# A graph network on one core: reading the numbers of four tiles with one register load

## The reference, cut to what matters

```python
edge_index = jnp.stack([src, dst])
x = _layernorm(x + _L0_gnn_ref(x, src, dst), axis=-1)                      # segment_sum(x[src], dst)
x = _layernorm(x + _L1_gnn_ref(x, edge_weight, src, dst, 10), axis=-1)     # ten passes of a segment_max
x = _layernorm(x + _L2_gnn_ref(x, edge_index, edge_weight, ...), axis=-1)  # three recurrent (LSTM-like) layers
x = _layernorm(x + _L3_gnn_ref(x, edge_index, edge_attr_4, ...), axis=-1)  # an edge MLP and a segment_sum
```

## Time and profile before

| | |
|---|---|
| median of three runs | 8305.31 us |
| profiled execution | 8315.25 us |
| its span, first to last instruction | 8313.5 us |
| PE matmul busy | 6032.0 us (73%) |
| PE weight load busy | 3014.6 us (36%) |
| DVE busy | 6536.5 us (79%) |
| ACT busy | 3628.6 us (44%) |
| POOL busy | 2284.8 us (27%) |
| instructions in the profile | 137264 |
| granted PE clock, mean | 0.929 |

### The profile page before, as it was taken

One profiled execution on the slowest core, in us unless ns is written; L12 is line 12 of the kernel. 1 busy time (PEld: TensorE's weight loads), 2 busy tenths in 40 slices (PEclk: granted clock), 3 DMA queues, 4 the chain that ended last, 5 costly groups with the idle time before them and its releaser, 6 DMA issues. The chain is left out here.

```text
span 8313.5 us, 137264 instructions
## 1 busy us (share of the span) xinstructions
PE 6032.0 (73%) x41218; PEld 3014.6 (36%) x41218; DVE 6536.5 (79%) x10561; ACT 3628.6 (44%) x4489; POOL 2284.8 (27%) x2074
## 2 busy tenths in 40 slices
PE   2111018879898989898989798989698989566665
PEld 2101014444343434343434343434354545233332
DVE  8999777678898989898989898988797979644443
ACT  0133102236565656565656565656343434233333
POOL 0000000003242324233334243333100000477775
PEclk9999999989999999999999999999799999777777
DMA  2000008867676767676767676767575767211111
GB/s 90 3 0 0 23 10 295 287 212 245 207 251 206 256 207 251 211 253 206 254 206 253 203 251 213 252 211 249 193 292 223 292 222 292 74 26 26 26 30 25
DMA packets 450935, 1460.66 MB, mean 176 GB/s; under 512 B 79869, under 2 KB 115365, under 8 KB 383008
## 3 DMA queue, kind: packets, MB, share of 16 engines
q1 hardware_dynamic: 228922, 1119.71, 39.4%
q10 hardware_dynamic: 157440, 298.89, 9.9%
q0 software_dynamic: 63872, 32.83, 2.3%
HBM read 1159.47 MB, written 291.94 MB: 175 GB/s over the span
## 5 line engine op out<-in xcount | busy, mean ns | idle before, releaser
L1464 PE MATMUL acc<-dst_hot,parts 128*128 128x512 bf16 x11600 | 2933.3, 382 | 337.2 <-issue 321.9
L1523 ACT ACTIVATE parts_out<-acc 96x1024 bf16<-96x1024 f32 x2320 | 2364.7, 1019 | 1713.2 <-PE acc L1475 1697.5
L1427 POOL DMA_INDIRECT group_best<-best_dram,best_row x1250 | 1408.2, 1127 | 2685.6 <-SPq L1390 2391.5
L1320 DVE TENSOR_SCALAR dst_hot<-dst_rows,node_f 128x2048 bf16<-128x2048 int16 x2910 | 2054.0, 740 | 115.5 <-PE acc L1475 108.3
L1464 PEld LDWEIGHTS acc<-dst_hot,parts 128*128 x11600 | 1047.8, 97 | 1544.8 <-issue 658.9
L924 POOL DMA_INDIRECT gathered<-table_dram,source_index x719 | 822.3, 1144 | 1525.1 <-POOLq L159 1306.3
L1475 PE MATMUL acc<-source,parts 128*128 128x128 bf16 x9280 | 909.8, 221 | 114.5 <-DMA source<-source_dram 109.1
L1475 PEld LDWEIGHTS acc<-source,parts 128*128 x9280 | 624.0, 98 | 757.5 <-issue 315.8
L1552 DVE TENSOR_TENSOR_SCAN best<-joined,best,risen 128x512 f32<-128x512 uint8 x570 | 727.5, 1276 | 0.7
L1546 DVE SCALAR_TENSOR_TENSOR risen<-rise,factor 128x512 f32<-128x512 f32 x580 | 400.9, 691 | 367.7 <-PE rise L1487 345.4
L362 PE MATMUL turned<-identity,ping 128*128 128x128 f32 x224 | 55.1, 427 | 771.5 <-DVEq L451 771.5
(11 more groups left out here) (386 smaller groups left out, 7802.5 us busy)
## 6 DMA issues: line engine op xcount, KB each, us to landing
dst_rows<-step_dst_dram SPq DMA_DIRECT2D x291, 1024.0 KB, 4.4
source<-source_dram SPq DMA_DIRECT2D x291, 1024.0 KB, 6.8
dst_kept_in<-dst_hot_dram SPq DMA_DIRECT2D x174, 1280.0 KB, 5.7
best_dram<-best_out ACTq DMA_DIRECT2D x580, 256.0 KB
factor<-step_weight_dram ACTq DMA_DIRECT2D x560, 256.0 KB
sources<-source_dram SPq DMA_DIRECT2D x174, 512.0 KB, 6.6
dst_hot_dram<-dst_kept SPq DMA_DIRECT2D x58, 1280.0 KB, 5.4
src_rows<-step_src_dram SPq DMA_DIRECT2D x58, 512.0 KB, 7.2
```

The costliest lines, as they stand in the source:

```text
L1320: nc.vector.tensor_scalar(hot[k % 2][b][:, :], index_rows[k // 2 % 2][:, k % 2, :], node_f[:, b:b + 1], None, ALU.is_equal).then_inc(hot_r ...
L1427: pool.indirect_dma_start(group_best[:, g, h, :], None, best_dram, bass.IndirectOffsetOnAxis(ap=best_row[:, i:i + 1], axis=0)).then_inc(en ...
L1464: nc.tensor.matmul(acc[n % 3][:, 0:TILE], blocks[b], hot[k % 2][b][:, q * TILE:(q + 1) * TILE], start=(b == 0), stop=(b == DST_BLOCKS - 1))
L1523: act.activation(moved[n % (2 * QUADS)][:, :], acc[n % 3][0:SPLIT, :], ACT.Copy).then_inc(tile_moved, 1)
```

## The change

In the first layer and in the recurrent layers the load of one number per tile becomes one load of four numbers per step. The four numbers stand 58 apart in `tile_info`, and four registers take them. The load for step k + 1 stands in tile 3 of step k, where the load for the next step's first tile stood before, between pair 0 and pair 1. Tiles 0, 1 and 2 have no load any more. The register operations stay, tile by tile. The two places are alike; the first:

```diff
-                    def load_number(m):
-                        k, q = divmod(m, QUADS)
-                        tile = q * STEPS1 + k
-                        number = pe.alloc_register(f"first{tile}")
-                        pe.load([number], tile_info[0:1, tile:tile + 1])
-                        numbers[m] = pe.snap(number, donate=True, min_val=0, max_val=DST_GROUPS << GROUP_BIT)
+                    def load_numbers(k):
+                        of_step = [pe.alloc_register(f"first{k}_{q}") for q in range(QUADS)]
+                        pe.load(of_step, tile_info[0:1, :].rearrange("o (q k) -> o k q", q=QUADS)[:, k, :])
+                        for q, number in enumerate(of_step):
+                            numbers[k * QUADS + q] = pe.snap(number, donate=True, min_val=0, max_val=DST_GROUPS << GROUP_BIT)
...
-                    load_number(0)
+                    load_numbers(0)
...
                                 if m + 1 < TILES:
                                     if j == 0:
-                                        load_number(m + 1)
+                                        if q == QUADS - 1:
+                                            load_numbers(k + 1)
                                         sources = sources_of(m + 1)
```

More of the change, by code:

```diff
@@ L1689, in _, with load_numbers @@
                         numbers = {}
[L1691 to L1696, removed]
+                        def load_numbers(k):
+                            of_step = [pe.alloc_register(f"tile{k}_{q}") for q in range(QUADS)]
+                            pe.load(of_step, tile_info[0:1, :].rearrange("o (q k) -> o k q", q=QUADS)[:, k, :])
+                            for q, number in enumerate(of_step):
+                                numbers[k * QUADS + q] = pe.snap(number, donate=True, min_val=0, max_val=DST_GROUPS << GROUP_BIT)
                         def sources_of(m):
```

## The result

The changed kernel took 8378.27 us in the median (8368.70 to 8392.83), the kernel before 8312.21 us beside it. The ratio is 1.0077 with a 95% interval of 1.0055 to 1.0099: slower by 66 us. The forecast was 8267 us, faster. The time lies on rival 1 (8380 us), which had a chance of 0.20, and 16 us above the range.

What follows compares the result with a forecast made beforehand. Waits between engines, not one full engine, bound the steps; PE's long loads set the first layer's pace. First layer -35 and recurrent layers -3 gave -38 us: 8277 profiled, 8267 us against the median; range 8238 to 8362.

Steps and rivals of the forecast that it cites:

- rival 1: Four reads run one after another, L = 1.2 us: recurrent layers +90 us, first layer -15, total 8380 us; chance 0.20.
- The length of the fused load: PE's load of four numbers: one round trip with little on top, below 0.6 us, between bounds of 301 and 1204 ns.
- The chain through the fused load: Recurrent step, tile 3's rows matmul to the next: 5.62 us plus load length L, costing nothing below L = 0.68 us.
- What the removed loads are worth there: Recurrent layers: taking three loads from each step gives about 0 a step, 3 us in all, bounds 0 and 10.
- the chain through DVE's one-hot and the second cast: Recurrent layers: from DVE's one-hot through PE's rows matmul, ACT's cast and DVE's L1847; said to set the 6.3 us step.
- The first layer: Removing PE's long loads takes a step from 8.64 to about 7.7 us in 42 steps: -35 us, ends 0 and 60.
- The landing of the index rows: First layer's next bound: rows issued 0.48 us after DVE begins land 7.2 us later, so a step takes at least 7.7 us.
- point of decision: Rival 1 decides from the load length where recurrent loss passes the first layer's gain of 35 us: 0.88 us.

Runs made afterwards that it cites:

- c_two_and_two: Against the changed kernel: two loads of two numbers, 58 apart, in tiles 1 and 3 of both stages, replace the load of four; 8330.10 us, ratio 1.0014.
- b_contiguous: Against the changed kernel: the four numbers of a step stand side by side in a copy of the row made in the index stage; 8241.72 us, ratio 0.9911.

## Why the prediction was wrong, point by point

**The length of the fused load** is the step that failed. The prediction left it between 301 and 1204 ns and took it "below 0.6 us, which is nearest to the row of 301 ns". Measured: 990 ns. The reason given, that four reads of one instruction can share the trip, holds only for four numbers that lie side by side and begin at a multiple of 16 bytes from the start of the copy (332 ns); 58 apart (990), 8 bytes apart (993) and shifted by 4 bytes (1002) they take the time of a trip each. The copy's own address stands in no trace, so that the group is one of 16-byte alignment in SBUF is likely and not shown. The diff showed the stride of 58, and the prediction did not ask what it costs. The Trainium skill's page Runtime: NRT & Kernel Launch (Instruction fetch mechanics) states about 200 ns for each register even in bulk, for loads from HBM. The loads here are from SBUF: the 230 ns for each further number of the strided loads are near that, the 332 ns for all four of a contiguous quad are not.

**The chain through the fused load** was right. The prediction had 5.62 us plus the length. After: 6.66 - 0.99 = 5.67. By its own formula the measured length gives (5.62 + 0.99 - 6.30) x 174 = 54 us; the layers grew by 59.1. With 525 ns nothing was lost against the kernel before, and from the changed kernel to four loads in a row the step followed the length, both as the formula has it.

**What the removed loads are worth there** was mis-sized. With the length back at 332 ns the three layers fell by 24 us, where the prediction took 3 and had 10 as the bound. It held that the chain through DVE's one-hot and the second cast sets the 6.30 us. The waits say otherwise: before the change DVE waits for the first cast in 55 steps of a layer and for the second in 3, so the chain through tile 3, tile 0 and the first cast held the step, and the load in tile 0 lay on it. Only with the contiguous quad does the second cast hold it, at 6.18 us.

**The first layer.** The forecast was -35 us, measured -14.1. The load in tile 3 does fall into the write, as the prediction said, but it lasts 2336 ns in the median, not 0.9 to 1.8 us, and the clock at the lower level for 48 us more had no term. Its sum was also loose at one place: PE at 6.8 to 7.7 us a step would give 0.9 to 1.8 us, and not "1.4 us or more". Rival 1 had the length right, 2 us or more; that its -15 us is what came is luck in part, since it is half of its own bound of -30, taken without a reason.

**The landing of the index rows** as the next bound had the right place and the wrong size. With the short load DVE does wait for them in 52 steps, but the layer takes 397 us, 82 less than before, where the prediction's end was 60. The 7.7 us of a step assumed that SP issues the rows 0.48 us after DVE began. When DVE stands waiting for rows, its one-hots of the step before are long made, and SP issues the next rows sooner: in the median 5.9 us after the start of a step, and they land 7.7 us later, for the step after the next. That is 13.6 us for two steps, and 397 / 58 = 6.8 us is what a step takes, at a DMA share of 0.96.

**The rivals.** Rival 1 gave the mechanism and the shape: the reads one after another, recurrent layers slower, first layer a little faster. That its total also fits (8380 us, and 8378 measured) is luck: it had +75 us from the two stages, which gave +45, and the rest came from stretches that it did not speak of. Its point of decision, a length of 0.88 us, lies between c_two_and_two and the changed kernel. It priced the recurrent layers at +90 with 1.2 us of length; they lost 59 with 0.99.

**What stays open.** The ten passes took between 4040.5 and 4109.3 us in traces whose instructions there are the same, a spread as large as the effect. No experiment was made on it, so the 12 us that they add in the changed kernel's trace are not explained, nor is how much of them is the kernel's and how much the execution's. In part it is the kernel's: b_contiguous gains 105.5 us in the two stages of its trace and 76.8 us in the median of four runs, and in c_two_and_two all ten runs are longer than its stages say. The effects above are read by stage for that reason. Why a shifted quad costs what four numbers apart cost was not taken further either, and what the lower clock costs the first layer was not separated from the stalls that it follows.

## What to carry to other kernels

When several small reads are fused into one instruction, ask for the length of the fused one before its count: here 3 of 4 loads went and the sequencer's time in loads fell only from 211 to 173 us in the recurrent layers, in blocks too long to be covered. Lay the values out side by side first, in groups that begin at multiples of 16 bytes from the start of the row (31 ns for three more numbers here, some 690 ns otherwise). Price a stall on the engine by the chain on which it lies: two loads of 0.525 us left the step of before as it was, 0.99 us in one piece cost 0.36 us of a step, and beyond that the step took on the whole of what was added. And look at who waits for whom before calling a removed wait worthless: the same four numbers in 0.33 us gave 24 us where 3 were taken.

## What the runs showed of the hardware

A register load of PE's sequencer from SBUF takes 301 ns for one number, 525 for two and 990 for four that lie apart, but 332 ns for a contiguous quad that begins at a multiple of 16 bytes from the start of its row, 1002 ns for one shifted by 4 bytes, and 592 ns for two unshifted quads. In the first layer, where one-hots are written from SBUF to DRAM and all transfers together make 289 GB/s, loads get longer (single ones up to 1929 ns in the earlier trace rows, a strided quad up to 4788 ns); with the larger of the two writes nearly gone the strided quad was at 1189 ns. Transfers into SBUF at a like rate, 292 GB/s in the recurrent layers of the earlier trace rows, stretched no load beyond 329 ns.
